# The last Runge-Kutta stage bank by bank, and ScalarE's eviction and drive pieces moved into stage 2

## The reference, cut to what matters

```python
def _derivative(q, p, drive, coupling, bias):
    i_couple = jnp.tanh(q) @ coupling.T
    dq = q - q ** 3 / 3.0 - p + drive + i_couple + bias
    dp = EPSILON * (q + ALPHA - BETA * p)
    return (dq, dp)
...
dq1, dp1 = _derivative(q, p, drive, coupling, bias)
dq2, dp2 = _derivative(q + 0.5 * DT * dq1, p + 0.5 * DT * dp1, drive, coupling, bias)
dq3, dp3 = _derivative(q + 0.5 * DT * dq2, p + 0.5 * DT * dp2, drive, coupling, bias)
dq4, dp4 = _derivative(q + DT * dq3, p + DT * dp3, drive, coupling, bias)
q_next = q + DT / 6.0 * (dq1 + 2 * dq2 + 2 * dq3 + dq4)
```

## Time and profile before

| | |
|---|---|
| median of 3 runs | 617.65 us (617.12 to 618.13) |
| the profiled execution | 617.41 us |
| its span, first to last instruction | 615.4 us |
| busy PE, PEld, DVE | 580.3 us (94%), 525.5 us (85%), 516.1 us (84%) |
| busy ACT, POOL | 401.7 us (65%), 255.7 us (42%) |
| chain that ended last, by engine | PE 63%, DVE 16%, ACT 14%, issue 4% |
| granted TensorE clock | 0.997 of full |

### The profile page before, as it was taken

The page is one execution under the profiler, slowest core; times in us unless marked ns, Lnnn a source line. Parts: engine busy times, 40 slices in busy tenths (PEclk is TensorE's granted clock), DMA queues, the critical chain, the costliest instruction groups (busy, mean ns, idle before and its releaser), DMA issues.

```text
span 615.4 us, 14209 instructions
## 1 busy us (share of the span) xinstructions
PE 580.3 (94%) x4918; PEld 525.5 (85%) x4918; DVE 516.1 (84%) x1544; ACT 401.7 (65%) x968; POOL 255.7 (42%) x401
## 2 busy tenths in 40 slices
PE   8899999999999879998888999999999999999997
PEld 7899999999999878887776888888888887888885
DVE  2776767776767768888988999999999999999996
ACT  2545454544445456575447888897888888788785
POOL 0333323232332353420144555555565565565550
PEclk9999999999999999998999999999999999999999
DMA  8400000000000000500000000000000000000001
GB/s 272 164 2 2 1 1 2 1 1 2 1 1 1 19 1 1 186 1 1 2 0 2 10 11 18 19 10 18 19 15 15 19 19 10 18 20 11 17 19 35
DMA packets 12517, 14.87 MB, mean 24 GB/s; under 512 B 1632, under 2 KB 10144, under 8 KB 12448
## 3 DMA queue, kind: packets, MB, share of 16 engines
q1 hardware_dynamic: 12448, 13.97, 6.7%
HBM read 9.78 MB, written 4.19 MB: 23 GB/s over the span
## 4 chain that ended last, share of the span: by engine, by line
PE 63%; DVE 16%; ACT 14%; issue 4%; SPq 1%; DMA 1%; POOL 0%; ACTq 0%; DVEq 0%
PE PS L451 18%; PE PS L313 16%; PE PS L336 12%; ACT q_s L756 4%; PE PS L503 3%; PE PS L524 3%; ACT k_s L737 2%; PE PS L429 2%; PE PS L389 2%; PE PS L487 2%; PE PS L372 2%; ACT big L669 2%; ACT q_s L798 2%; DVE h_s L1056 1%; DVE big L938 1%
## 5 line engine op out<-in xcount | busy, mean ns | idle before, releaser
L451 PE MATMUL PS<-k_s,h_s 128*128 128x128 f32 x1024 | 160.7, 285 | 4.5 <-DVE PS L1036 1.9
L451 PEld LDWEIGHTS PS<-k_s,h_s 128*128 128x128 f32 x1024 | 131.7, 191 | 21.7 <-DVE PS L1044 9.7
L313 PE MATMUL PS<-part 128*128 128x256 f32 x900 | 115.6, 286 | 0.7 <-issue 0.7
L313 PEld LDWEIGHTS PS<-part 128*128 128x128 f32 x900 | 109.8, 191 | 0.9 <-issue 0.9
L737 ACT ACTIVATE k_s<-h_s 128x128 f32<-128x128 f32 x256 | 68.8, 305 | 41.1 <-DVE h_s L1056 33.7
L336 PE MATMUL PS<-big,wrk 128*128 128x128 f32 x744 | 88.4, 275 | 3.0 <-DVE big L895 3.0
L336 PEld LDWEIGHTS PS<-big,wrk 128*128 128x128 f32 x744 | 85.8, 192 | 3.6 <-DVE big L895 3.6
L1204 POOL COPY h_s<-big 128x256 f32<-128x256 f32 x32 | 21.4, 670 | 131.0 <-DVE big L895 131.0
L451 PE MATMUL PS<-h_s 128*128 128x128 f32 x384 | 74.2, 275 | 0.0
L451 PEld LDWEIGHTS PS<-h_s 128*128 128x128 f32 x384 | 58.3, 192 | 0.0
L634 ACT ACTIVATE big<-big 128x256 f32<-128x256 f32 x32 | 13.3, 416 | 65.6 <-DVE big L877 65.6
(11 more groups left out here) (184 smaller groups left out, 1270.9 us busy)
## 6 DMA issues: line engine op xcount, KB each, us to landing
out<-q_s SPq DMA_DIRECT2D x32, 128.0 KB, 1.7
x_s<-in_xT SPq DMA_DIRECT2D x14, 256.0 KB, 6.1
k_s<-in_wgT SPq DMA_DIRECT2D x1, 832.0 KB, 5.8
k_s<-in_wuT SPq DMA_DIRECT2D x1, 832.0 KB, 7.4
k_s<-in_wih SPq DMA_DIRECT2D x3, 256.0 KB, 4.4
wrk<-in_whh SPq DMA_DIRECT2D x3, 256.0 KB, 4.8
h_s<-in_wdT SPq DMA_DIRECT2D x1, 768.0 KB, 6.4
x_s<-in_xT SPq DMA_DIRECT2D x4, 128.0 KB, 3.6
```

Source lines behind the costliest of these rows:

```text
L313: r = pe.matmul(p, y, x, start=i == 0, stop=i == len(passes) - 1)
L451: return pe.matmul(PS[:, m, 0:128], w, x, start=False, stop=True, skip_group_check=True)
```

## The change

ScalarE's eviction of `po` moves from the end of the step to behind the copy of `px` in slot 2, and waits for a new semaphore `s_h2` instead of the product and transpose counts. The drive of the next four steps is made in four pieces of 256 columns, one in slot 2 of each step. On VectorE the scales of the middle activations become two one-column instructions: the rounding scale ahead of the results of slot 2, and the output's scale (`s_h2`) ahead of those of slot 3; the reciprocal stands behind the first of the results. `seed_4` and `nexts` are called for one bank at a time, so that result 0, seed 0, result 1, seed 1 follow each other; t3 and t4 both stand ahead of the last cubic term. TensorE's products of slot 3 are written out in another order, with a wait for each bank's seed and each half's tanh. The transposes into `px` wait for the eviction of the same step's bank.

```diff
--- before.py
+++ after.py
@@ -176,7 +176,7 @@
         I_at = lambda t: drive[:, t // 4 % 2, :, t % 4 * B:(t % 4 + 1) * B]
         th = [k_s[:, 1, 3072 + 256 * r:3328 + 256 * r] for r in range(2)]
         x1n = [k_s[:, 1, 1792 + 256 * r:2048 + 256 * r] for r in range(2)]
-        drive_done = lambda t: 2 * (t // 4) + 4 if t else 2
+        drive_done = lambda t: 4 * (t // 4) + 4 if t else 2
         by416 = lambda a: a.rearrange("p (s n) -> p s n", s=2)
         q_at = lambda i, a, n=1: sm_[:, 8 * (i % 4) + a:8 * (i % 4) + a + n]
         h_at = lambda i, a, n=1: sm_[:, 32 + 8 * (i % 4) + a:32 + 8 * (i % 4) + a + n]
@@ -212,7 +212,7 @@
         s_q0, s_cb, s_mag, s_cp = sem("s_q0"), sem("s_cb"), sem("s_mag"), sem("s_cp")
         s_x1t, s_x1k, s_dr = sem("s_x1t"), sem("s_x1k"), sem("s_dr")
         s_th, s_sq, s_w, s_ps, s_next, s_seed = (sem(n) for n in ("s_th", "s_sq", "s_w", "s_ps", "s_next", "s_seed"))
-        s_t3, s_t4, s_p, s_q = (sem(n) for n in ("s_t3", "s_t4", "s_p", "s_q"))
+        s_t3, s_t4, s_p, s_q, s_h2 = (sem(n) for n in ("s_t3", "s_t4", "s_p", "s_q", "s_h2"))
         s_u3, s_uz, s_v1, s_W3, s_WZ, s_dq, s_t1, s_t2 = (
             sem(n) for n in ("s_u3", "s_uz", "s_v1", "s_W3", "s_WZ", "s_dq", "s_t1", "s_t2"))
         s_turnq, s_turnqi, s_gate, s_up, s_turnh, s_down = (
@@ -526,7 +526,17 @@
                     r.then_inc(s_gate, 1)
 
 
-                coupled(4 * t + 3, id_z3, qs[1])
+                slot, w = 4 * t + 3, th[1]
+                pe.wait_ge(s_seed, 2 * slot + 1)
+                add(0, id_z3, cm(qs[1], 0))
+                pe.wait_ge(s_th, 2 * slot + 1)
+                add(0, coupU[:, 0, 0:128], cm(w, 0))
+                pe.wait_ge(s_seed, 2 * slot + 2)
+                add(1, id_z3, cm(qs[1], 1))
+                add(1, coupU[:, 0, 128:256], cm(w, 0))
+                pe.wait_ge(s_th, 2 * slot + 2)
+                add(0, coupU[:, 1, 0:128], cm(w, 1)).then_inc(s_ps, 1)
+                add(1, coupU[:, 1, 128:256], cm(w, 1)).then_inc(s_ps, 1)
                 if t == 0:
                     keep_warm(7, 3)
                 if t >= 2:
@@ -535,8 +545,8 @@
                         pe.wait_ge(s_add, 16)
                     else:
                         pe.wait_ge(s_x1k, i)
-                    if i >= 2:
-                        pe.wait_ge(s_osc, i - 1)
+                    if i:
+                        pe.wait_ge(s_osc, i)
                     for k in range(2):
                         r = pe.transpose(cm(px, k), x_s[:, k, i * B:(i + 1) * B], ident[:, :])
                     r.then_inc(s_x1t, 1)
@@ -775,6 +785,16 @@
                     ac.wait_ge(s_x1t, i + 1)
                     ac.wait_ge(s_down, i + 1)
                     ac.activation(x1n[i % 2], px, ACT.Copy).then_inc(s_x1k, 1)
+                    if i >= 2:
+                        ac.wait_ge(s_st[i % 2], 16 * (i // 2))
+                    ac.wait_ge(s_h2, i + 1)
+                    ac.activation(ob[i % 2], po, ACT.Copy, scale=h_at(i, 2)).then_inc(s_osc, 1)
+                n, j = t // 4 + 1, t % 4
+                if n < 8:
+                    if n >= 2:
+                        ac.wait_ge(s_seed, 8 * (4 * n - 5) + 4)
+                        ac.wait_ge(s_WZ, 4 * n - 4)
+                    drive_block(n, j % 2, j // 2 * 256, j // 2 * 256 + 256)
 
 
                 stage(4 * t + 3)
@@ -783,19 +803,6 @@
                     ac.wait_ge(s_tq, i + 1)
                     ac.wait_ge(s_gate, i + 1)
                     ac.activation(by416(sg), pg, ACT.Silu, scale=q_at(i, 2)).then_inc(s_sg, 1)
-                n, k = divmod(t + 3, 4)
-                if k < 2 and n < 8:
-                    if n >= 2:
-                        ac.wait_ge(s_seed, 8 * (4 * n - 5) + 4)
-                        ac.wait_ge(s_WZ, 4 * n - 4)
-                    drive_block(n, k)
-                if t >= 3:
-                    i = t - 3
-                    if i >= 2:
-                        ac.wait_ge(s_st[i % 2], 16 * (i // 2))
-                    ac.wait_ge(s_down, i + 1)
-                    ac.wait_ge(s_x1t, min(i + 2, T))
-                    ac.activation(ob[i % 2], po, ACT.Copy, scale=h_at(i, 2)).then_inc(s_osc, 1)
 
             def middle(i, a=0, b=NI):
                 ac.wait_ge(s_s2, i + 1)
@@ -1036,22 +1043,21 @@
                 ve.scalar_tensor_tensor(PS[:, m, 0:128], cm(qn[t % 2], m), (1 + 2 * A * kap) / (2 * c4), cm(W3, m),
                                         ALU.mult, ALU.add).then_inc(s_seed, 1)
 
-            def seed_4(t):
+            def seed_4(t, m):
                 ve.wait_ge(s_dq, t + 1)
                 ve.wait_ge(s_WZ, t + 1)
-                for m in range(2):
-                    ve.wait_ge(s_next, 8 * t + 5 + m)
-                    ve.scalar_tensor_tensor(PS[:, m, 0:128], cm(dq, m), 1 / c4, cm(WZ, m), ALU.mult,
-                                            ALU.add).then_inc(s_seed, 1)
+                ve.wait_ge(s_next, 8 * t + 5 + m)
+                ve.scalar_tensor_tensor(PS[:, m, 0:128], cm(dq, m), 1 / c4, cm(WZ, m), ALU.mult,
+                                        ALU.add).then_inc(s_seed, 1)
 
             def cubic(slot, src):
                 s = slot % 4
                 ve.wait_ge(s_sq, slot + 1)
                 ve.scalar_tensor_tensor(w_, sqP, cube[s] * own[s], src, ALU.subtract, ALU.mult).then_inc(s_w, 1)
 
-            def nexts(slot, dst):
+            def nexts(slot, dst, ms=(0, 1)):
                 ve.wait_ge(s_w, slot + 1)
-                for m in range(2):
+                for m in ms:
                     ve.wait_ge(s_ps, 2 * slot + m + 1)
                     ve.scalar_tensor_tensor(dst(m), PS[:, m, 0:128], of_ps[slot % 4], cm(w_, m), ALU.mult,
                                             ALU.subtract).then_inc(s_next, 1)
@@ -1115,26 +1121,29 @@
                     ve.wait_ge(s_hN, 2 * i + 2)
                     ve.tensor_reduce(h_at(i, 0), hN[i % 2], X, ALU.max, apply_absolute_value=True).then_inc(s_mxh, 1)
                 cubic(4 * t + 2, qs[1])
-                nexts(4 * t + 2, lambda m: cm(qs[2], m))
-
-
-                seed_4(t)
                 if t >= 2:
                     ve.wait_ge(s_mxh, i + 1)
-                    ve.scalar_tensor_tensor(h_at(i, 1, 2), wide(h_at(i, 0), 2), TINY, wvec[:, 3:5], ALU.max,
-                                            ALU.mult).then_inc(s_thh, 1)
+                    ve.tensor_scalar(h_at(i, 1), h_at(i, 0), TINY, 1.0 / 127.0, ALU.max, ALU.mult).then_inc(s_thh, 1)
+
+
+                nexts(4 * t + 2, lambda m: cm(qs[2], m), (0,))
+                if t >= 2:
+                    ve.wait_ge(s_thh, i + 1)
+                    ve.reciprocal(h_at(i, 4), h_at(i, 1)).then_inc(s_s2, 1)
+                seed_4(t, 0)
+                nexts(4 * t + 2, lambda m: cm(qs[2], m), (1,))
+                seed_4(t, 1)
                 if t < T - 1:
                     ve.wait_ge(s_t2, t + 1)
                     ve.wait_ge(s_next, 8 * t + 4)
                     ve.scalar_tensor_tensor(t3, t2, horner[2], qs[1], ALU.mult, ALU.add).then_inc(s_t3, 1)
-                cubic(4 * t + 3, qs[2])
-                if t < T - 1:
                     ve.wait_ge(s_t3, t + 1)
                     ve.wait_ge(s_next, 8 * t + 6)
                     ve.scalar_tensor_tensor(t4, t3, horner[3], qs[2], ALU.mult, ALU.add).then_inc(s_t4, 1)
+                cubic(4 * t + 3, qs[2])
                 if t >= 2:
                     ve.wait_ge(s_thh, i + 1)
-                    ve.reciprocal(h_at(i, 4), h_at(i, 1)).then_inc(s_s2, 1)
+                    ve.tensor_scalar(h_at(i, 2), h_at(i, 1), wmean[:, 2:3], None, ALU.mult).then_inc(s_h2, 1)
                 nexts(4 * t + 3, lambda m: PS[:, m, 128:256])
                 for m in range(2):
                     ve.wait_ge(s_next, 8 * t + 7 + m)
```

## The result

The changed kernel takes 624.0 us (median of 4 runs, 623.5 to 625.57) where the kernel before takes 617.89 (4 runs beside it): a ratio of 1.0105, 95% interval 1.0088 to 1.0123. It is slower by 1%. The profiled execution took 624.14 us against 617.41.

A forecast was written before the change was run, and what follows sets the result against it. VectorE's own instruction order was taken to bound the step: +0.19 − 0.03, taken as 0.17 us over 29 steps, adds 4.9 to 617.65, giving 622.6 us, first and last steps cancelling; 8-in-10 range 616.8 to 625.3.

The forecast's parts named there:

- VectorE's own order sets the step, and ScalarE's handover does not: Second recurrence's steps: VectorE's instruction order decides the change's worth; ScalarE's tanh 0.15 us earlier at the border gains little.
- Rival 1: Step border: ScalarE's handover is the bound, so some 28 steps gain 0.15 us each, 613.4 us; chance 0.10.
- 0.13 us for a late wait among three: Last-stage seeds on VectorE: each starts 0.13 us after its result's end, the last-written of three waits being late.
- rival 2: Last-stage seeds: waits cost only 0.03 us each, no change, 616.5 to 617.6 us; one bank only 619.7; chance 0.14 for both.
- The sum: Full step: +0.19 VectorE order, −0.03 stage 2 pair, taken as 0.17 us; 29 steps give +4.9 us.
- The column of starts: VectorE's estimated starts from the third cubic term to the next step's seed: 3.72 us against 3.53, costing 0.19 a step.
- the short account beside it: VectorE's last stage: 0.26 us spent on two seed waits, 0.12 on t4, 0.17 saved from the gap TensorE's bank 1 made.
- the pair of stage 2: VectorE's stage 2 seeds, at 496.43: earlier tanh and transposes remove a 0.03 us gap per step.
- Steps 0 and 1 give back 0.1 each: First two steps, waiting for TensorE without scaling work: the new product order gives back about 0.1 us each.
- Rival 3: TensorE's bank 1, the late Silu or small instructions become late, each up to 0.1 us a step: about 627; chance 0.08.

The follow-up runs named there:

- act_moves_alone: Kernel before with only ScalarE's part of the change (eviction, four drive pieces in stage 2, TensorE's wait for it): 617.7 us against 617.53, ratio 0.9995.
- the run that takes the price away: Changed kernel with the last stage's seeds writing their wait for the result just ahead first of three: 618.61 us, ratio 1.0018.
- pe_order_alone: Kernel before with only TensorE's new order of the last stage's products: 617.71 us, ratio 1.0006.
- mended_pool_later: The mended kernel with POOL's first product of a step (v1) waiting until both first seeds are written: 629.18 us, ratio 1.0196.
- after_t4_behind_cubic: Changed kernel with t4 put back behind the last cubic term: 622.92 us, ratio 1.0075.
- the last run: The mended kernel with both middle scales in one two-column instruction ahead of stage 3's results, as in the kernel before: 620.46 us, ratio 1.0046.
- the mended kernel: Changed kernel: seeds' late wait first, last-stage result 0 carrying TensorE's wait, output's scale ahead of last cubic term, t4 behind, old order in steps 0 to 2: 617.52 us.

## Why the prediction was right

- *VectorE's own order sets the step, and ScalarE's handover does not.* Right: act_moves_alone took nothing off. Rival 1 fell with it.
- *0.13 us for a late wait among three.* Right to the rounding, twice a step, and the run that takes the price away gives 5.0 to 5.4 us back; rival 2 is what that run shows, and it needed the edit to come true. The Trainium skill's page "VectorE: DVE Perf Modes" (The DRAIN you can't avoid) has the semaphore of a chained instruction free; here it costs 0.03 when it rides in the instruction and 0.10 or 0.13 when it is handled ahead.
- *The sum.* 0.17 us a step was too small; 28 steps show 0.225. (The column of starts gives the 0.19 that the sum uses; the short account beside it, 0.26 and 0.12 spent and 0.17 saved, adds up to 0.21.) Two terms of it were mis-sized. The chain from the cubic term to the next seed is 3.76 and not 3.72: what follows a seed starts 0.21 later and not 0.20, and the cubic term 0.34 behind t4, hundredths that add up to 0.04. And I had credited 0.03 for the pair of stage 2, which didn't come: its second start (500.70) is still bound by TensorE, whose last record of bank 1 ends at 500.66; that run begins behind the same seed as before.
- *Steps 0 and 1 give back 0.1 each.* Wrong in sign: +0.29 and +0.11, and step 2 +0.75. The new product order by itself gave nothing back there: in pe_order_alone these two steps took 10.03 and 8.93 against 9.98 and 8.89. What failed besides is that I looked for POOL's difference only in a full step. Step 0's VectorE has little else to do, so POOL is late there, and behind a waiting seed 0 stood result 1.
- *The distance of 1.4 us from 622.6* is partly luck. The loop alone, by this pair of executions, is 7.56 us longer, where I had 4.9. Where the loop begins is nothing of the change, and it lies between 307.34 and 309.75 in the profiled executions of this document.
- *Rival 3 (each of the other engines late by up to 0.1)* did not occur: in the usual steps no gap on VectorE names TensorE (the one at the pair of stage 2 is 0.03, as before), and ScalarE's drive piece ends at 502.99, ahead of the tanh at 503.01, which waits for its input anyway.

## What to carry to other kernels

When an instruction waits for several semaphores, write the one that comes last as the first, so that it rides in the instruction; on VectorE here that was worth 0.10 us a time and decided the change. Splitting a pair of independent instructions into dependent steps takes away the cover that each gave the other, so count the exposed latency before the gain. A chain of waits names one path: before crediting a shorter piece of it, look whether the engine that it feeds has any gap at all.

## What the runs showed of the hardware that was not expected

A VectorE instruction with two inputs in SBUF that begins while POOL is in one of its own can take longer, and then ends with POOL's or up to 0.16 us after it: a 128-column seed took 0.73 instead of 0.29 (mended_pool_later), 0.38 to 0.41 at v1, and a two-column scaling 0.34 instead of 0.15. The seeds ended 0.14 to 0.16 after POOL's instruction, whether that had one input (v1: 501.60 + 0.38 = 501.98 against 501.84) or two (t1: 502.93 against 502.78). A seed that starts close to POOL's end loses nothing: in after_t4_behind_cubic it began 0.07 before v1's end and took its 0.29. Instructions with one input in PSUM showed nothing of it. The third cubic term of the kernel before starts inside POOL's difference (498.19 in the earlier trace rows, 498.12 to 498.85 in the earlier trace rows) and takes 0.41, where the next one outside it takes 0.42; in the last run a result (L1065 at 502.18) started inside the POOL instruction that had held the scaling (L1287) and took its 0.28.

A one-column product whose factor is read from SBUF took 0.21 in the mended kernel and moved the cubic term behind it by 0.12, against 0.15 and 0.08 for the reciprocal of the earlier trace rows. The square that this cubic term waits for had ended 0.08 ahead of it, and it follows such a square after 0.03 where nothing else holds it, so the 0.12 is the product's. POOL was idle then. In the changed kernel the product takes 0.21 too, but there the cubic term's end sets the start of the next instruction, and its 0.12 says nothing. No run shows what of this comes from the factor's place.
